# A vision block with attention and routed experts on one core: other queues for the row transfers, expert weights copied by DMA, and the last image's bookkeeping moved

## What is computed

```python
xn = (x - mu) * rsqrt(var + EPS) * ln_g + ln_b            # over the whole image
Q, K, V = (dwconv3x3(pointwise(xn)) for each of q, k, v)   # 8 heads of 24 channels
attn = softmax(K^T Q / alpha); x = w_f @ (V attn) + b_f + xn   # attention over channels
t = to_tokens(x)                                           # 16 x 1024 rows of 192
n1 = layernorm(t)
t = t + causal attention(n1, W_qkv, W_proj, b_proj)        # 6 heads of 32, the projection applied twice,
                                                           # within each 1024-row image
n2 = layernorm(t)
probs = softmax(n2 @ gate_w + gate_b); top 2 of 4 experts, shares renormalised
y_e = gelu(n2 @ w1[e] + b1[e]) @ w2[e] + b2[e]             # 192 -> 768 -> 192
t = t + share_1 * y_e1 + share_2 * y_e2
```

## Time and profile before

| | |
|---|---|
| median of 3 runs (lowest to highest) | 3534.71 us (3533.25 to 3537.79) |
| the profiled execution: time / span | 3531.58 us / 3529.7 us |
| PE busy, share of the span | 3125.3 us, 89% |
| PE weight loads | 2381.5 us, 67% |
| DVE busy | 2337.5 us, 66% |
| ACT busy | 1836.2 us, 52% |
| POOL busy | 1145.8 us, 32% |
| mean granted clock of PE | 0.959 |
| bytes moved | 414.50 MB, 117 GB/s |

### The profile page before, as it was taken

The page is one execution under the profiler, slowest core; times in us unless marked ns, Lnnn a source line. Parts: engine busy times, 40 slices in busy tenths (PEclk is TensorE's granted clock), DMA queues, the critical chain, the costliest instruction groups (busy, mean ns, idle before and its releaser), DMA issues. The chain is left out here.

```text
span 3529.7 us, 73345 instructions
## 1 busy us (share of the span) xinstructions
PE 3125.3 (89%) x26642; PEld 2381.5 (67%) x26642; DVE 2337.5 (66%) x5867; ACT 1836.2 (52%) x3868; POOL 1145.8 (32%) x1702
## 2 busy tenths in 40 slices
PE   4899898898998989989889899866999999999995
PEld 1666666566666666666656666645888888888884
DVE  3767777677676776776767767683565665665654
ACT  0547456365474563644636547443555555555553
POOL 2131312303213133031230321303454545545554
PEclk9999999999999999999999999987999999999997
DMA  7545445444364453534644445402233333333332
GB/s 175 134 112 157 108 123 144 116 133 119 111 170 109 117 138 110 150 101 124 158 112 120 126 112 163 138 21 60 82 109 102 115 96 116 103 106 110 109 104 88
DMA packets 243804, 414.50 MB, mean 117 GB/s; under 512 B 69847, under 2 KB 156311, under 8 KB 242377
## 3 DMA queue, kind: packets, MB, share of 16 engines
q1 hardware_dynamic: 207854, 343.47, 35.9%
q0 software_dynamic: 31488, 64.53, 6.4%
q10 hardware_dynamic: 4107, 1.81, 0.3%
HBM read 242.82 MB, written 117.71 MB: 102 GB/s over the span
## 5 line engine op out<-in xcount | busy, mean ns | idle before, releaser
L1010 DVE TENSOR_REDUCE minus_max<-ps 128x1 f32<-128x128 f32 (+7 forms) x768 | 570.6, 749 | 228.1 <-PE ps L1754 224.3
L1451 ACT ACTIVATE p_sb<-ps,minus_max 128x128 f32<-128x128 f32 (+7 forms) x768 | 567.6, 742 | 94.0 <-DVE minus_max L1010 91.2
L1764 PE MATMUL ps<-ident,p_sb 128*128 128x128 f32 x3456 | 542.6, 282 | 42.7 <-ACT p_sb L1451 17.8
L1338 DVE TENSOR_TENSOR g_lo<-g,g_hi 128x512 fp32r<-128x512 f32 x402 | 312.5, 777 | 327.6 <-ACT g_hi L1575 327.6
L1574 ACT ACTIVATE g<-ps,bcur 128x512 f32<-128x512 f32 x402 | 276.8, 689 | 466.6 <-PE ps L1949 466.6
L1752 PE MATMUL ps<-KS,QS 96*128 96x512 f32 (+3 forms) x1152 | 404.2, 410 | 56.4 <-ACT p_sb L1451 40.5
L1764 PEld LDWEIGHTS ps<-ident,p_sb 128*128 128x128 f32 x3456 | 376.0, 143 | 96.3 <-issue 33.5
L710 POOL COPY inverse_wide<-inverse_sums 128x192 f32<-128x192 f32 x128 | 44.7, 349 | 1214.5 <-DVE inverse_sums L1031 1214.5
L1965 PE MATMUL ps<-w_all,g_hi 128*128 x1608 | 436.5, 353 | 0.0
L1465 ACT ACTIVATE PT<-ps 128x512 f32<-128x512 f32 (+3 forms) x640 | 340.8, 532 | 159.7 <-PE ps L1764 151.7
L770 POOL CAST cur<-w_all 128x384 fp32r x536 | 281.2, 557 | 392.6 <-DVE g_lo L1338 392.3
(11 more groups left out here) (279 smaller groups left out, 5663.1 us busy)
## 6 DMA issues: line engine op xcount, KB each, us to landing
ring<-padded_scratch SPq DMA_DIRECT2D x576, 204.0 KB
routed_rows<-zero_rows SPq DMA_DIRECT2D x67, 384.0 KB, 5.1
xgt<-routed_rows SPq DMA_DIRECT2D x67, 384.0 KB, 4.0
expert_rows<-y_rows SPq DMA_DIRECT2D x67, 384.0 KB, 2.6
padded_scratch<-xpad SPq DMA_DIRECT2D x32, 435.0 KB, 3.5
x_sb<-x SPq DMA_DIRECT2D x16, 768.0 KB
KS<-QKh SPq DMA_DIRECT2D x128, 96.0 KB, 2.5
KS<-QKh SPq DMA_DIRECT2D x64, 192.0 KB, 3.5
```

Of the source, the lines that this page charges most:

```text
L1010: v.tensor_reduce(nmx[:, qc, h:h + 1], score_place(n), AX, ALU.max, negate=True).then_inc(mx_sb, 1)
L1338: v.tensor_tensor(g_lo[:, n % 2, :], g32[:, n % 2, :], g_hi[:, n % 2, :].bitcast(F32), ALU.subtract).then_inc(lo_sb, 1)
L1451: a.activation(p_sb[n % NP][:, 0:P * (qc + 1)], score_place(n), ACT.Exp, bias=nmx[:, qc, h:h + 1], accum_out=ls[:, qc, h:h + 1]).then_inc( ...
L1764: last = t.transpose(bank(pass_bank(piece))[:, P * k:P * (k + 1)], p_sb[n % NP][:, P * (k0 + k):P * (k0 + k + 1)], ident[:, :])
```

## The change

- In each image POOL's 16 sends of the image before are placed anew: 6 before the first `token_rstd`, 4 before the second, 2 behind it, and 4 behind the `QS` transfers of wave 0. Of wave 0, POOL now issues all six `QS` transfers (it was three), SP three fewer.
- PE runs `last_heads` for chunks 0 to 3 in a row, and the input part of chunk 5 behind them.
- `row_ranks` on DVE is two operations on 256 elements in place of eight on 64.
- Last image: POOL splits the experts' weights, two or three pairs of operations behind each `inverse_wide` of chunks 2 to 6 (`split_behind`). The second normed rows of chunks 0 to 3 are written behind unit 40, into a buffer of their own that lies over the first half of `QS`. After the attention the route skips them, has `gate_weights` behind `slots`, and `shares` last.
- Second phase: SP fills `cur` with one DMA of 1536 KB from `w_all` for each block, behind the `up` of the block that used the buffer. POOL has no weight copies; it copies the biases, and fetches a unit's 8 gathers in one go, one block after the last answers.

```diff
@@ rows, semaphores @@
-        xhat2 = at("xhat2", [P, NC, C], F32, R + 16 * K)
+        xhat2_at = [at(f"xhat2_{n}", [P, NC, C], F32, R + 16 * K * (1 - n)) for n in range(2)]
+        ahead_of = at("ahead_of", [P, NC, E, NC], F32, routed_at[0] - 2 * 4 * NC * E * E)
+        def rows_of(i):
+            return xhat2_at[i + 1 == B]
@@ SP, in the loop over images @@
-                load_queries(sp, 0, 0, 0, QKh)
-                load_queries(sp, 0, 0, 2, QKh)
                 sp.wait_ge(qk_lo, NQ * i + PAIR_GROUPS)
                 for j in range(2):
                     load_keys(sp, 0, j, 2, QKl)
-                load_queries(sp, 0, 0, 1, QKl)
@@ SP, second phase @@
+            def load_weights(r):
+                expert = sp.value_load(tab[0:1, r:r + 1], min_val=0, max_val=E - 1)
+                if r >= 2:
+                    sp.wait_ge(up_ps, J * (r - 1))
+                sp.dma_start(cur[r % 2][:, :].bitcast(F32), w_all[:, bass.ds(expert, 1), 0:4 * W1L].rearrange("p e f -> p (e f)").bitcast(F32)
+                             ).then_inc(cur_ld[r % 2], 16)
...
             sp.wait_ge(t_st, 16 * B)
+            sp.wait_ge(w_split, 1)
+            sp.wait_ge(table_sb, 1)
+            load_weights(0)
             sp.wait_ge(sent, SENT * B)
             for r in range(3):
                 load_block(r)
             for r in range(NBLK):
+                if r + 1 < NBLK:
+                    load_weights(r + 1)
                 if r + 1 in UNIT_OF:
                     load_tokens(UNIT_OF[r + 1])
@@ POOL @@
+            def split_weights(hi, lo, src, last=False):
+
+                g.tensor_copy(hi, src).then_inc(w_hi, 1)
+                halves[0] += 1
+                pool.wait_ge(w_hi, halves[0])
+                ins = g.tensor_tensor(lo, src, hi.bitcast(F32), ALU.subtract)
...
+            def split_behind(qc):
+
+                if qc == 2:
+                    pool.wait_ge(w_ld["w1a"], 16)
+                    pool.wait_ge(w_ld["w1b"], 16)
+                    split_first(0, 0)
+                    split_first(0, 1)
+                if qc == 3:
+                    pool.wait_ge(w_ld["w2"], 16 * E)
+                    split_second(0)
+                    split_first(1, 0)
+                if qc == 4:
+                    split_first(1, 1)
+                    split_second(1)
+                if qc in (5, 6):
+                    split_first(qc - 3, 0)
+                    split_first(qc - 3, 1)
+                    split_second(qc - 3)
...
             for i in range(B):
                 unpad_image(pool, i)
                 if i:
-                    send(i - 1, 0, 5)
+                    send(i - 1, 0, 3)
                 token_rstd(i, 0)
                 if i:
-                    send(i - 1, 5, 7)
+                    send(i - 1, 3, 5)
                 token_rstd(i, 1)
                 if i:
-                    send(i - 1, 7, NC)
+                    send(i - 1, 5, 6)
                 pool.wait_ge(qk_hi, NQ * i + PAIR_GROUPS)
-                load_queries(g, 0, 1, 0, QKh)
-                load_queries(g, 0, 1, 2, QKh)
+                for j in range(2):
+                    load_queries(g, 0, j, 0, QKh)
+                    load_queries(g, 0, j, 2, QKh)
                 pool.wait_ge(qk_lo, NQ * i + PAIR_GROUPS)
-                load_queries(g, 0, 1, 1, QKl)
+                for j in range(2):
+                    load_queries(g, 0, j, 1, QKl)
+                if i:
+                    send(i - 1, 6, NC)
...
-                pool.wait_ge(lo_sb, J * r + 3)
-                copy_weights(r + 1, expert, (4, 5))
-                pool.wait_ge(lo_sb, J * r + 4)
-                copy_weights(r + 1, expert, (6, 7))
+            copy_biases(0)
+            for r in range(NBLK):
+                if r + 1 < NBLK:
+                    copy_biases(r + 1)
                 if r + 2 in UNIT_OF:
-                    fetch(UNIT_OF[r + 2], (0, 1))
+                    fetch(UNIT_OF[r + 2])
@@ DVE @@
-                for e in range(E):
-                    last = v.tensor_tensor(
...
-                    link(v.tensor_reduce(rank[:, :, e], src, AX, ALU.add))
+                link(v.tensor_tensor(ahead_of[:, :, :, :],
+                                     chosen[:, :, :].rearrange("p m e -> p e m").unsqueeze(1).to_broadcast([P, NC, E, NC]),
+                                     before_k[:, :, :].unsqueeze(2).to_broadcast([P, NC, E, NC]), ALU.mult))
+                link(v.tensor_reduce(rank[:, :, :], ahead_of[:, :, :, :], AX, ALU.add))
...
-                    if i + 1 == B and 20 <= n < 20 + len(splits):
-                        if n == 20:
-                            for name, count in (("w1a", 1), ("w1b", 1), ("w2", E)):
-                                dve.wait_ge(w_ld[name], 16 * count)
-                        split(n - 20)
+                    if i + 1 == B and n == 40:
+                        second_normed(i, 0)
...
-            for step in range(7):
-                route(B - 1, step)
+            gating(B - 1)
+            second_normed(B - 1, 1)
+            routing(B - 1)
+            row_ranks(B - 1)
+            open_blocks(B - 1)
+            block_rows(B - 1)
+            slots(B - 1)
+            gate_weights(B - 1)
+            block_table(B - 1)
             finish_table()
+            shares(B - 1)
@@ PE @@
-                last_heads(i, 0)
-                last_heads(i, 1)
+                for k in range(4):
+                    last_heads(i, k)
                 input_and_first_heads(i, 5)
-                for k in range(2, 6):
+                for k in range(4, 6):
                     last_heads(i, k)
...
-                    pe.wait_ge(cur_sb, 8 * (r + 1))
+                    pe.wait_ge(cur_ld[r % 2], 16 * (r // 2 + 1))
```

77 lines of the change are left out of this document (23 added, 54 removed).

## The result

The changed kernel takes 3473.2 us (median of 4 runs, 3471.77 to 3482.61) against 3536.25 us for the kernel before in the same comparison: a ratio of 0.9826, 95% interval 0.9804 to 0.9847. It is faster, but by 63 us where 114 were forecast, and 3473.2 lies 5 us above the range. The profiled execution took 3472.44 us with a span of 3470.6 us, 59.1 less than the span of before.

The account below looks back on a forecast made before the run. It took POOL's queue in the images, DVE's weights wait and splits in the last image, and POOL's late weight copies in the blocks as bounds. Terms -75 + 5 - 13 + 30 - 19 - 3 - 39 = -114 gave 3420 us, range 3375 to 3468.

Parts of the forecast that it names:

- Sends behind the variances, and PE's new order: Images 1 to 15: POOL's first power follows the variances at once, PE's wait before the transposes shrinks; 4.8 us an image, -75.
- The second power: Images: the second power has the seventh to tenth sends ahead and comes 0.35 us late, 15 times; +5 us.
- The `QS` transfers: Images, wave 0: with POOL issuing all six, nearly all of PE's 14.6 us wait for the last piece goes; -13 us.
- What is late next: Images: POOL reaches the first `inverse_wide` 1.1 to 2.8 us late and PE stops there; 2.0 taken, 15 times, +30 us.
- Last image: Chunks 3 to 5: DVE loses the weights wait and 24 split operations; -19 us, between -22 and +5.
- After the attention: Only two operations between counts and block opening: 3.3 us sooner, with the sends; first weights copied while POOL issues; -3 us.
- Blocks: Second phase: without POOL's weight copies PE's 38.9 us of waits go, if the DMA is in time; -39 us.
- A: Images: POOL takes it back, two gaps, wave 1 late too, 4.5 us an image instead of 2.0; 3462 us, chance 0.15.
- B: Images: POOL is not late, no gap after seven sends, clock stays up in the transposes; 3369 us, chance 0.15.
- C: Last image: POOL's splits hold up DVE, each for its own length, 42 us lost; 3460 us, chance 0.08.
- D: Blocks: weights' DMA takes 24 us and sets the block at 23 instead of 16.0 us; 3919 us, chance 0.04.
- E: Blocks: PE's 23 waits are its own register load at a block's start and stay; 3457 us, chance 0.04.

Follow-up runs that it names:

- e11: Changed kernel with the last four sends behind the first `inverse_wide` (3364.1 us), given PE's old order of the last heads: 3377.8 us.
- e10: Changed kernel with the last four sends behind the first `inverse_wide` (3364.1 us), three even-head `QS` transfers of wave 0 back on SP: 3403.7 us.
- e2: Changed kernel (3473.2 us) with the sends where they stood before the change, all else as changed: 3432.8 us.
- e4: Changed kernel (3473.2 us) with the three even-head `QS` transfers of wave 0 on SP again: 3414.3 us.
- e5: Changed kernel (3473.2 us) with the 24 split operations of the last image back on DVE: 3489.8 us.
- e7: Changed kernel (3473.2 us) with the transfer of block 0's weights moved behind the last send and block 0's rows: 3477.6 us.
- e6: Changed kernel (3473.2 us) with the blocks' weights copied by POOL again, in eighths between the gathers: 3515.0 us.
- e8: Changed kernel with last four sends behind the first `inverse_wide` (3364.1 us), POOL's last-image splits one chunk later, expert 3 behind the last power: 3359.5 us.
- e3: Changed kernel (3473.2 us) with POOL's second output bias addition behind the first `inverse_wide`: 3445.2 us.

## Why the prediction was wrong

**What bounds the kernel** was read rightly: the queue on POOL in the images, the weights and splits in the last image, POOL's copies in the blocks.

**Sends behind the variances, and PE's new order, -75.** Right as far as it goes. The first two rows of the table of stretches give 0.93 + 4.25 = 5.2 us an image for the forecast 5.0, and PE waits 0.6 us as forecast. e11 prices PE's order at 14 us of it (11 forecast).

**The second power, +5.** In image 8 it came 0.68 us late instead of 0.35, and no wait of PE shows it.

**The `QS` transfers, -13.** The wait is gone, and with the clock of the old place the third row gives 1.43 us. But e10 shows that the move is worth 40 us where POOL has room: the forecast priced the wait alone, not the slow stretch behind it. In the kernel before, where the wait was shorter (0.85 us an image against 1.2), the 1.8 us an image from e2 and e11 make it an estimated 27 us.

**What is late next, +30.** This is the step that failed. Its mechanism is right: POOL is late at the first `inverse_wide`, where it had idled for 6.58 us. Its size was 4.86 + 1.98 = 6.84 us an image instead of 2.0, some 100 us in all instead of 30. Two things were missed. First, the sum of issues took each at its bare length, 26.7 us after the power. In the means over images 1 to 14 the work up to the twelfth send ends at 11.4, just as summed; then the six transfers take 4.1 us for 3.3, the four sends 5.5 for 5.0, the other six transfers 5.5 for 3.3, and POOL arrives at 30.0. The sums were ready at 24.8, not at 25.6. So it is late by 5.2 us, beyond the given bound of 2.8. (Image 8, shown above, is the mildest: stops of 0.64 and 1.04 among the transfers, a gap of 0.90 among the sends, 29.13 against 24.76, late by 4.4.) The largest part is the stops among the last six transfers, 2.2 us, where all nine transfers of before met 0 to 0.5 us of stops in an image; e4, with nine again, has 0.8 to 2.1. Why POOL stops there no run shows. Second, the slow clock. The prediction had seen it at the old place (1.97 us for eight transposes instead of 1.09) and set it down as an uncounted gain of up to 0.9 us. It didn't ask what a stop at the new place would do to the matmuls behind it, and there it costs 2.0 us an image. The two errors come to 4.8 us in each of 15 images, 73 us, more than the whole miss of 55 us in the span; the small gains above and image 0 give part of it back. Image 0, in which little was forecast, ended 6.4 us sooner. 2.9 of that are there before the first power, in the waits for the first loads, and among the other kernels here image 0 ended anywhere from 200.0 to 207.9: mostly scatter.

**Last image, -19.** -22.9 in chunks 2 to 5. e5 puts 17 us on the splits and leaves 6 to the shorter wait for the weights.

**After the attention, -3.** The slots came 3.3 us sooner, as summed. The sends gave 2.4 back, since the transfer of block 0's weights stretched their gap from 1.95 to 4.20 us (e7). The prediction said that the transfer runs while POOL issues, and didn't ask what it does to the sends.

**Blocks, -39.** -37.3, and the waits are gone to 0.2 us (e6).

**The rivals.** A, "POOL takes it back", is what happened: stops in the transfers in every image, a second gap in 5 of 14, nothing left of the 6.58 us. It said 4.5 us an image, 3462 us; with the 2.0 us of clock behind the stop it is 6.8. Its chance of 0.15 was too low for a forecast that left POOL with less than no slack: the forecast itself had POOL late, so each optimistic length in its queue went straight into the time, 15 times. B falls with the gap of 1.96 us behind the seventh send. C does not come in the attention (30.84 us for chunks 2 to 5, where image 14 took 31.98 before), and e8 shows the same lock at work where DVE reads SBUF twice. D and E fall with 7.1 us and e6.

## What to carry to other kernels

When work is moved down a queue, add up that queue to the first instruction behind it for which someone waits, with the stops and gaps that its issues show in the trace, and not with their bare lengths; two moves that each gain alone can cancel if both are paid ahead of the same instruction. A stop of PE in a dense stretch costs the wait and the slow matmuls behind it, so count it at the price of both, at the old place and at the new; where the stop is down to 1.5 to 2.8 us, as in e4, the second part came in some images and not in others, and the runs scattered. The cheapest place for work that nobody waits for is right behind an instruction for which someone does.

## What the hardware showed that was not expected

- **A short stop can cost more than itself.** In e10 a stop of 1.64 us, with PE busy for 12.9 of the 14 us before it, brought the clock to 0.50 for the 4 us from 1233 on, and 16.4 us of such waits in images 1 to 14 came with a kernel 40 us slower. In the changed kernel the stop of 4.52 us brought it to 0.53 for 10 us. In e3 stops of 1.8 to 5.0 us still did in every image; in e4 stops of 1.5 to 2.8 us did in 6 of 14, and not the longest ones alone, and the time of such a kernel scatters (3399.5 to 3429.6).
- **The gap in the sends is not a constant.** In the last image of before it was 1.95 us in front of the 8th and of the 15th send, 0.30 in front of all others. In the changed kernel the 15th send of an image, with other issues between, had 0.8 to 1.7 in 5 of images 1 to 14 (0.90 in image 8) and 0.30 in the others, and the 8th of the last image had 4.20 while a transfer of 1536 KB was under way.
- **DVE and POOL on SBUF.** A DVE operation of 0.19 us took up to 1.68 beside POOL's 1.8 us operations, and four scalings 4.50 instead of 1.24; a reduction in between took its 0.19.
